# Two half-batches of a cross attention, put half a turn apart in the written order of four engines

## What is computed

```
qh, kh, vh = heads(x @ Wq.T + bq), heads(ctx @ Wk.T + bk), heads(ctx @ Wv.T + bv)   # 16 heads of 16
scores = einsum('bhqd,bhkd->bhqk', qh, kh) * 0.25
scores = where(mask[:, None] == 0, -1e9, scores)
probs  = softmax(scores, axis=-1)                         # over 77 keys
out    = einsum('bhqk,bhkd->bhqd', probs, vh)             # 256 queries for each of the 16 batches
x      = layernorm(x + concat(out) @ Wo.T + bo)
```

## Time and profile before

| | us |
|---|---|
| median of three runs | 1551.7 (1550.95 to 1552.25) |
| the profiled execution, its own time | 1550.95 |
| its span, from the first to the last instruction | 1549.2 |
| cross attention, main part (first block exponential to the last copy of logits) | 786.7 to 1002.0 |
| PE, DVE, ACT, POOL busy over the whole span | 1318.7, 873.2, 890.5, 713.8 |
| mean granted TensorE clock | 0.922 |

### The profile page before, as it was taken

One profiled execution on the slowest core, in us unless ns is written; L12 is line 12 of the kernel. 1 busy time (PEld: TensorE's weight loads), 2 busy tenths in 40 slices (PEclk: granted clock), 3 DMA queues, 4 the chain that ended last, 5 costly groups with the idle time before them and its releaser, 6 DMA issues. The chain is left out here.

```text
span 1549.2 us, 31029 instructions
## 1 busy us (share of the span) xinstructions
PE 1318.7 (85%) x10439; PEld 1114.1 (72%) x10439; DVE 873.2 (56%) x1806; ACT 890.5 (57%) x2018; POOL 713.8 (46%) x792
## 2 busy tenths in 40 slices
PE   5899999999999999999689999714999999998100
PEld 4788888888888888887567777504888888888100
DVE  3345555554454555545378888486555555566446
ACT  4677777777777777777237777501555544555101
POOL 2244444444444444445347777303545454454564
PEclk9999999999999999999789999855999999999555
DMA  3300000000000000000123443202455445554334
GB/s 129 77 15 22 28 29 29 22 29 22 22 29 22 29 29 22 29 22 22 45 66 104 111 112 105 71 17 97 134 180 165 149 142 175 162 184 138 96 112 124
DMA packets 127907, 120.61 MB, mean 78 GB/s; under 512 B 42498, under 2 KB 108650, under 8 KB 127786
## 3 DMA queue, kind: packets, MB, share of 16 engines
q1 hardware_dynamic: 120970, 100.42, 20.9%
q0 software_dynamic: 6816, 18.62, 4.4%
HBM read 83.93 MB, written 28.26 MB: 72 GB/s over the span
## 5 line engine op out<-in xcount | busy, mean ns | idle before, releaser
L293 POOL TENSOR_SCALAR_AFFINE_SELECT a_decay<-a_decay 128x256 f32<-128x256 f32 x256 | 114.7, 452 | 260.4 <-ACT a_decay L373 258.8
L496 DVE TENSOR_TENSOR a_probs<-a_ps_s,a_decay 128x384 f32<-128x384 f32 x256 | 131.6, 553 | 158.4 <-PE a_ps_o L676 147.4
L302 POOL TENSOR_TENSOR a_key_sum<-a_probs 128x256 f32<-128x256 f32 x128 | 94.2, 736 | 170.3 <-DVE a_probs L496 158.3
L336 ACT ACTIVATE a_qk_exp<-a_ps_qk 128x512 f32<-128x512 f32 x128 | 76.5, 598 | 137.7 <-PE a_ps_qk L582 130.6
L582 PE MATMUL a_ps_qk<-a_xT_hi,a_w_hi 128*128 128x256 f32 x512 | 144.8, 283 | 3.6 <-ACT a_qk_relu L337 3.6
L489 DVE SCALAR_TENSOR_TENSOR a_qk<-a_qk_exp,a_qk_relu 128x512 f32<-128x512 f32 x128 | 89.1, 696 | 97.3 <-ACT a_qk_relu L337 97.3
L582 PE MATMUL a_ps_qk<-a_xT_hi,a_w_lo 128*128 128x256 f32 x512 | 143.8, 281 | 0.0
L582 PE MATMUL a_ps_qk<-a_xT_lo,a_w_hi 128*128 128x256 f32 x512 | 143.6, 281 | 0.0
L1760 POOL TENSOR_TENSOR e_gu_lo<-e_gu_raw,e_gu_hi 128x2048 fp32r<-128x2048 f32 x23 | 106.8, 4643 | 79.7 <-ACT e_gu_hi L1780 79.7
L657 PE MATMUL a_ps_s<-a_qk 64*128 64x256 f32 (+1 forms) x1024 | 132.2, 338 | 0.6 <-DVE a_probs L496 0.4
L1753 POOL DMA_INDIRECT e_x_in<-x_rows,e_index x78 | 74.8, 959 | 123.1 <-DVE e_index L1856 106.1
(11 more groups left out here) (282 smaller groups left out, 4016.0 us busy)
## 6 DMA issues: line engine op xcount, KB each, us to landing
e_gu_raw<-in_L_ffn_gate_w SPq DMA_DIRECT2D x23, 512.0 KB
e_gu_raw<-in_L_ffn_up_w SPq DMA_DIRECT2D x23, 512.0 KB
e_dn_raw<-in_L_ffn_down_w SPq DMA_DIRECT2D x23, 512.0 KB
y_sorted<-e_y_out SPq DMA_DIRECT2D x16, 512.0 KB
a_x_in<-in_x SPq DMA_DIRECT2D x16, 256.0 KB, 2.7
a_x_res<-in_x SPq DMA_DIRECT2D x16, 256.0 KB, 2.7
x_rows<-a_x SPq DMA_DIRECT2D x16, 256.0 KB, 2.1
x_bo_rows<-a_x_bo SPq DMA_DIRECT2D x16, 256.0 KB, 2.1
```

The source lines that it names most:

```text
L293: pool.affine_select(out=d, in_=d, compare_op=ALU.is_ge, fill=0.0, base=0, pattern=[[0, 2], [1, P]], channel_multiplier=-1)\
L302: pool.tensor_tensor(key_sum[:], probs[:, :, P:N], probs[:, :, N:TRI], ALU.add).then_inc(keys_summed, 1)
L336: act.activation(qk_exp[:], ps_qk[:], ACT.Exp)
L496: vec.tensor_tensor(probs[:, h, :], ps_s[h][:, 0:TRI], decay[h][:], ALU.mult)\
```

## The change

It moves steps within the rounds and adds or removes none. Block 1 of a batch is put half a round behind block 0: what ran as the pair (b+1, 0), (b+1, 1) on GpSimd and VectorE is split, so that block 1 of batch b is read out, shifted and exponentiated in round b. On ScalarE the exponential of block 0 of batch b+1 is now the last step of round b, and `normalise(b - 2)` stands between two copies near the round's start. On TensorE `project_q` and `turn_probs` are mixed in another way, and the second `score` is the last step of the round.

```
@@ gpsimd @@
             def sequence(b, par, turn):
+                shift(b, par, 1)
                 weigh(b, par, 0)
                 weigh(b, par, 1)
                 if has(b, 1):
                     shift(b + 1, 1 - par, 0)
-                    shift(b + 1, 1 - par, 1)
                 if has(b, 2):
                     mask_to_bias(b + 2, par)
...
             shift(0, 0, 0)
-            shift(0, 0, 1)
             all_sequences(pool, sequence)
@@ scalar @@
             def sequence(b, par, turn):
-                if has(b, -1):
-                    keep_pT(b - 1, 1 - par, 1, (0,))
                 if has(b, 1):
                     keep_xT(b + 1)
                 if has(b, -1):
-                    keep_pT(b - 1, 1 - par, 1, (1,))
-                exponentials(b, par, 0)
+                    keep_pT(b - 1, 1 - par, 1, (0, 1))
+                if has(b, -2):
+                    normalise(b - 2)
                 if has(b, -1):
                     keep_pT(b - 1, 1 - par, 1, (2,))
-                exponentials(b, par, 1)
                 if has(b, 1):
                     keep_q(b + 1)
+                exponentials(b, par, 1)
                 if has(b, -1):
                     keep_oT(b - 1)
-                if has(b, -2):
-                    normalise(b - 2)
-                keep_pT(b, par, 0, (0,))
+                keep_pT(b, par, 0, (0, 1))
                 if has(b, -2):
                     keep_x2T(b - 2)
-                keep_pT(b, par, 0, (1, 2))
+                keep_pT(b, par, 0, (2,))
                 if has(b, -2):
                     keep_logits(b - 2)
+                if has(b, 1):
+                    exponentials(b + 1, 1 - par, 0)
...
             keep_q(0)
+            exponentials(0, 0, 0)
             all_sequences(act, sequence)
             keep_pT(B - 1, (B - 1) % 2, 1, range(NG))
-            keep_oT(B - 1)
             normalise(B - 2)
             keep_x2T(B - 2)
             keep_logits(B - 2)
+            keep_oT(B - 1)
             normalise(B - 1)
@@ vector @@
             def sequence(b, par, turn):
+                keep_scores(b, par, 1)
                 sums(b, par, 0)
                 sums(b, par, 1)
                 if has(b, 1):
                     keep_scores(b + 1, 1 - par, 0)
-                    keep_scores(b + 1, 1 - par, 1)
                 if has(b, -1):
                     add_residual(b - 1)
                     statistics(b - 1)
...
-            keep_scores(0, 0, 1)
             all_sequences(vec, sequence)
@@ tensor @@
             def sequence(b, par, turn):
-                if has(b, -1):
-                    turn_probs(b - 1, 1 - par, 1, (0,))
                 if has(b, 1):
                     turn_x1(b + 1)
                 if has(b, -1):
-                    turn_probs(b - 1, 1 - par, 1, (1, 2))
+                    turn_probs(b - 1, 1 - par, 1, (0, 1))
                 if has(b, 1):
                     project_q(b + 1)
                 if has(b, -1):
+                    turn_probs(b - 1, 1 - par, 1, (2,))
                     weigh_values(b - 1, 1 - par, turn - 1 + par)
                 if has(b, 1):
                     score(b + 1, 1 - par, turn + par, 0)
+                turn_probs(b, par, 0, (0, 1))
+                if has(b, -2):
+                    turn_x2(b - 2)
+                turn_probs(b, par, 0, (2,))
                 if has(b, -1):
                     project_o(b - 1)
-                turn_probs(b, par, 0, (0,))
+                if has(b, -2):
+                    route(b - 2)
                 if has(b, 1):
                     score(b + 1, 1 - par, turn + par, 1)
-                if has(b, -2):
-                    turn_x2(b - 2)
-                turn_probs(b, par, 0, (1, 2))
-                if has(b, -2):
-                    route(b - 2)
...
             weigh_values(B - 1, (B - 1) % 2, (B - 1) // 2)
-            project_o(B - 1)
             turn_x2(B - 2)
             route(B - 2)
+            project_o(B - 1)
             turn_x2(B - 1)
             route(B - 1)
```

4 lines of the change are left out of this document (1 added, 3 removed).

## The result

| | before | after |
|---|---|---|
| median, first set of runs | 1551.33 (1548.68 to 1552.25) | 1578.91 (1576.73 to 1579.9) |
| median, later set (beside e8 to e12) | 1549.67 (1544.03 to 1553.26) | 1580.27 (1578.61 to 1583.95) |
| profiled execution and its span | 1550.95, 1549.2 | 1584.93, 1583.2 |
| cross attention, first to last instruction on its `b_` tiles | 748.38 to 1001.77: 253.4 | 748.46 to 1035.34: 286.9 |

The changed kernel is slower, by a ratio of 1.0179, 95% interval [1.0162, 1.0197]; in the later set 1.0202 [1.0184, 1.022]. The stage is 33.5 us longer in the profiled execution, and 31.7 longer in that of the later set.

The account below looks back on a forecast made before the run. TensorE was taken to bound the old round, a cross-engine loop the new one; 23.4 + 0.4 + 4.6 + 4 = 32.4 us on 1550.95 gave 1583.3, as a median 1584, range 1574 to 1600 for 8 in 10.

Parts of the forecast that it names:

- TensorE bounds the old round, at 11.97 us and 0.70 of waits: Cross attention before: TensorE sets the 12.67 us round, 11.97 its own plus 0.70 of waits for ScalarE copies.
- The loop: Chain from exponential 0 through ScalarE, VectorE, GpSimd back to it next batch: 14.41 us a round, +23.4 over 13 rounds.
- ScalarE's half: Part of the loop on ScalarE, from exponential 0 to the end of exponential 1: 7.26 us.
- The other half: Sum, reciprocal, next scores 0 and maximum on VectorE, then GpSimd's shift, back to exponential 0: 7.15 us with both 0.03 gaps.
- The clock, +4, bounds 0 and 20: TensorE's long wait halves its clock in some four of 13 rounds, about 1 us each: +4, bounds 0 and 20.
- The start, +0.4: Stage start, up to exponential 0 of batch 2: 814.7 or 813.2 against 813.64, taken as +0.4 us.
- The end, +4.6: Stage end: last round +1.9 to +3.1, steps now ahead of the last project_o +2.1; together +4.6 us.
- The sum: Rounds, start, end and clock: 23.4 + 0.4 + 4.6 + 4 = 32.4 us on the profiled execution's 1550.95.
- the waits go and nothing takes their place: Rival: TensorE still sets the round at 11.97 without waits on ScalarE's copies; -9.1 us, 1543; 4 in 100.
- VectorE's own loop at 12.97: Rival: only maximum 1, shift, exponential 1, sum 1 count, without ScalarE's queue; 12.97 a round, 1560; 7 in 100.
- A clock that stays down: Rival: TensorE's clock falls nearly every round and stays down through most; rounds about 16.5, 1605, throughout 1670; 10 in 100.
- No change: Rival: time as before, for which the loop would have to be 12.5 us long; 3 in 100.

Follow-up runs that it names:

- e8: Kernel before, with TensorE's score 1 moved behind the second group of transposes and ScalarE's keep_q ahead of exponential 1; 1545.14 us, ratio 0.9976.
- e12: The changed kernel run again, unedited, on the chip of the later set; 1580.27 us, ratio 1.0202 to before.
- e1: Changed kernel plus two dead 128x512 copies on ScalarE each round, between exponential 0 and exponential 1, ahead of normalise; 1593.69 us, ratio 1.0279 to before.
- e2: Changed kernel plus two dead 128x512 copies on ScalarE each round, behind exponential 1 and the copy of b_oT; 1580.28 us, ratio 1.0188 to before.
- e9: Changed kernel with one group of block 1's transposes done five times, 16 more matmuls a round in TensorE's longest wait; 1567.63 us, ratio 1.0199 to before.
- e7: Changed kernel with the last project_o and keep_oT back in their old places behind the last round; 1565.27 us, ratio 1.0186 to before.
- e4: Changed kernel with normalise(b - 2) moved back behind keep_oT(b - 1) on ScalarE; 1588.37 us, ratio 1.0249 to before.
- e5: Kernel before with only the change's GpSimd and VectorE orders, TensorE and ScalarE as before; 1554.27 us, ratio 1.012 to before.
- e10: Kernel before with all 16 cross attention rounds written out, no program loop, same order on every engine; 1544.69 us, ratio 0.9971.
- e11: Kernel before with the edits of both e8 and e10; 1541.14 us, ratio 0.995.
- e6: Kernel before with only the change's TensorE order within the rounds, its end and the other engines as before; 1566.13 us, ratio 1.019 to before.

## Why the prediction was right

*TensorE bounds the old round, at 11.97 us and 0.70 of waits; right, as far as e8 shows it.* In e8, within the old order, one of the three waits of the earlier trace rows is gone, the 0.26 for `b_x2T`, and the round falls by 0.28, to 12.39:

```profile
881.53 0.97 PEld L1314 LDWEIGHTS b_ps_m<-b_rwT,b_x2T 128*128 128x128 f32 x8
```

*The loop; right, shown by e1, e2 and e9.* 14.41 was forecast; it is 14.53 in the program's loop and 14.22 in the rounds that are written out. ScalarE's half was put at 7.26, with the 0.03 behind it at 7.29, and is 880.07 - 872.79 = 7.28. The other half was put at 7.12 without that 0.03 and is 887.32 - 880.07 = 7.25. The 0.13 stand in the step from sum to scores 0: 1.76 instead of 1.64, since VectorE's first scores instruction comes 0.29 after the reciprocal's start and not 0.17, in the program's loop only. The prediction took all its rows from the program's loop and priced every round by them. The 13 rounds without clock falls were put at 187.3; e9 shows 188.1, as ten rounds are 0.13 longer than forecast and three 0.19 shorter.

*The clock, +4, bounds 0 and 20; mis-sized.* There were four falls in 13 rounds, as was guessed, but at 0.3 to 0.4 each: the rounds with a fall are 14.83 twice and 14.64 twice, where e9 has 14.54 and 14.23. That is 1.3 us in all (189.4 - 188.1), a third of the 4. That it was four falls is luck: the number was a guess, and e2 has two in its rounds, e1 six. One of them, TensorE and the windows around it:

```profile
889.08 2.67 PE L1242 MATMUL b_ps_m<-b_xT,b_wT 128*128 128x256 f32 x8 [1.92 <-ACT b_xT L992]
```
```profile
885.00:890.25 5.25, 3.33 (x33) 2.82 (x34) 4.98 (x11) 3.07 (x7) 3.30 (x3) 1.00 0.57 172
890.25:893.66 3.41, 3.41 (x14) 2.12 (x14) 1.22 (x2) 3.18 (x10) 3.41 (x2) 0.50 0.40 121
893.66:900.00 6.34, 6.34 (x60) 5.00 (x58) 4.83 (x8) 3.34 (x6) 3.22 (x3) 1.00 0.07 6
```

The fall begins 1.2 us into `project_q`, which takes 2.67 instead of 1.99 and stays within the slack of 0.9; what gets through is the rest of the slow stretch in `weigh_values`, for which scores 0 wait 0.33 on VectorE (896.66, against a slack put at 1.3). In e1, where a round is 1.04 longer with the same work for TensorE, the six falls make no round longer. The step that failed is the price of one fall: it was worked out as though the clock were down for the whole of `project_q` and more. The wait stands where it was put, ahead of `project_q`, but it is shorter than the 2.44 forecast: 23.2 / 12 = 1.9 us on the load side, from 1.07 to 2.43 in the 13 rounds, and 1.92 on the multiply side in the round above.

Every round has the wait, but only four of 13 have the clock at 0.50, in both traces of the changed kernel at the same places. The Trainium skill (TensorE: Matmul & The Clock Gate, section HAM oscillation) tells of a kernel that was throttled in every turn, by waits of 3 to 5 us. The waits here are 2.43 at the longest, so no run here repeats that case; with them the clock fell in some turns and in none of the traces in each.

*The start, +0.4; too low by 0.2 to 0.75.* Counted from the stage's own start, the exponential of batch 2 comes 1.15 us later than before (814.87 - 748.46 against 813.64 - 748.38), 0.6 in e12.

*The end, +4.6; too low.* It is 6.9 in the profiled execution (31.28 us from the last exponential of block 0 to the last logits, 24.39 before), 5.4 in e12. The 1.5 between the two traces are one row, the last `project_o`, of the changed kernel and of e12:

```profile
1023.72 3.50 PE L1294 MATMUL b_ps_o<-b_wT,b_oT 128*128 128x256 f32 x8 [0.75 <-ACT b_oT L1021]
```
```profile
1022.84 1.99 PE L1294 MATMUL b_ps_o<-b_wT,b_oT 128*128 128x256 f32 x8 [0.75 <-ACT b_oT L1021]
```

In the one the clock is at 0.50 (from 1023.37), in the other at 1.00 there. That the clock can fall behind the last round, where nothing covers it, was left out of the term for the end. Of the rest, e7, whose last `project_o` takes 1.99 too, has 28.2 - 24.4 = 3.8, so the moved `project_o` costs 5.4 - 3.8 = 1.6 and not 2.1 (its own terms in the prediction add up to 2.2), and the last round itself 3.8 instead of 1.9 to 3.1.

*The sum.* 32.4 was forecast for the profiled execution; the stage grew by 33.5, and by 31.7 in e12. That the sum is within 1.1 of the stage's growth is in part luck, since its errors cancel: 0.8 too little for the 13 rounds, 2.7 too much for the clock, 0.75 too little at the start and 2.3 at the end. The median went up by 27.6 in one set and by 30.6 in the other. The changed kernel's runs behind the 27.6 have no trace, so where their 5 us less than 1584 lie can't be shown; the traces point outside the stage. What is left of the span without it is 1295.8 us before and 1296.3 after, but 1293.4 in e12 and 1287.4 to 1293.6 in the four traces of e1 to e4, where no line outside the stage differs. The routing takes 34.7 us in every trace; the experts take 399.6 to 405.2 and the combination 88.1 to 103.5. What makes these two vary is not settled.

*The rivals.* That the waits go and nothing takes their place falls with e1. VectorE's own loop at 12.97 falls with e1, where copies on ScalarE make the round 1.04 longer; e5, where ScalarE keeps its old order, has rounds of 12.94 to 13.19 at two places where they are written out; that loop may bind there, but it is not the longest in the changed kernel. A clock that stays down falls with the windows, and e9, without a fall, has the round of 14.54. No change falls with the time.

## What to carry to other kernels

Where engines work in written order, look for the longest chain that leads from a step back to the same step one turn later, through every engine's queue, before believing that the busiest engine sets the pace; here, spreading a pair of steps half a turn apart put all that then stood between them into such a chain. When a loop is cut, price the next longest too: e4 took `normalise` out of one loop, closed a second one as long, and lost 7 to 10 us on the changed kernel, more than the second loop explains. And to find out whether a step is in the loop, add dead work there and, once more, just outside: here 1.16 us of copies made the round 1.04 us longer inside and 0.01 outside.

## What the runs showed of the hardware

- The same rounds are longer in the program's loop than written out: 12.67 against 12.57 in the old order (e10, all engines' instructions in the same order) and 12.39 against 12.28 in e8's (e11). In the new order it is 14.53 against 14.22, there between rounds at other places of the stage. In e9, which has no falls, the 0.3 of the new order stand at three places: VectorE's scores begin 0.29 instead of 0.17 us after the reciprocal's start and take 0.06 longer, and ScalarE waits 0.17 ahead of the last step of `normalise` (the row at 891.35 above), where the written-out round has no wait, as in the changed kernel:

```profile
832.97 1.09 ACT L1040 ACTIVATE b_x<-b_resid,b_shift,b_rstd 128x256 f32<-128x256 f32 x2
```

  What in the loop causes it wasn't tried apart.
- TensorE's granted clock read 0.50 for 3.41 us behind weight-load waits of 2.16 to 2.43 us ahead of `project_q` (830.84, 889.08, 947.50, 991.39) and stayed at 1.00 behind others of 2.39 and 2.43 us (874.55, 932.97), at the same four places in both traces of the changed kernel. With the wait filled (e9) there was no fall in these rounds.
- The kernel before took 1536.18 us on one chip and 1549.7 to 1551.3 in the other sets, some 14 us apart. Its trace is not from that chip; but in the four traces from there (e5, e6, e7, e9) the last stage, the combination, takes 88 us, and 99 to 104 in the others. The changed order has the same rounds on it (e7, 14.54).
